# A choice of engine for each group in the token-wise half of a two-layer kernel

## The chip, the cores and the metric

One core of a Trainium2 chip runs the whole program. The metric is the device time of one launch in microseconds (us). Of the engines, PE is TensorE, DVE is VectorE, ACT is ScalarE, POOL is GpSimd and SP is SyncE, which only starts DMAs here.

## What is computed

Two transformer layers over 2048 tokens of 128 features, in float32. Between x and the output stand four residual blocks:

```python
x = x + attention(layernorm(x))        # 16 heads of 64, a dilated local mask
x = x + fp4_ffn(layernorm(x))          # gate, up and down, each with inputs and weights quantised
x = x + l1_attn(layernorm(x))          # see below
x = x + l1_ffn(layernorm(x))           # r, k, v with a mix of each token and the one before it

def fp4_quant_dequant(x):              # blocks of 16
    scale = max(max(abs(xb)) / 6, 1e-12)
    return GRID[searchsorted(MID, abs(xb / scale))] * sign(xb) * scale

# l1_attn: h1 = norm1_w * rms(x); q, k, v, a, g = in_proj(h1)
# q = rms over groups of 8; k = tanh(k); a = clip(sigmoid(a + 2), 0.6, 0.9995)
# states: a recurrence over the tokens with a and k * v, computed in chunks of 64
# y = sigmoid(g) * (q * states) + (1 - sigmoid(g)) * v; x = x + RES * out_proj(y)
# h2 = norm2_w * rms(x); x + RES * proj(silu(fc(h2)))
# l1_ffn: out = sigmoid(xr @ W_r) * (relu(xk @ W_k) ** 2 @ W_v)
```

## The kernel before

The program has two halves. The first is the attention block: 32 units (8 head pairs by 4 windows of 512 tokens) in a software pipeline over all engines. The second, the token-wise half, computes the other three blocks. It is cut into four groups g = 0 to 3 of 512 tokens (four tiles of 128), and every group runs the same chain of some 130 named steps, one or a few instructions each. A step is named in the code by a short name, and `h1(2)` is step h1 of group 2.

**Order.** There is no loop over the groups. Each engine has one list, written out by hand or by a planner, in which the steps of the four groups stand in the order in which the engine issues them, interleaved with the last attention units (28 to 31). An engine runs its list strictly in order: a step that waits holds up all behind it. The table `STEPS` names for each engine and group the steps in their order, so that `wait_for(e, name, g)` can turn a step's name into a semaphore's value. There is one semaphore for each engine and group.

**Steps, in the order of the data.** x1 adds attention's output; bn0 and ag0 take mean and variance; rs0 (POOL, four small instructions) makes the inverse deviation and, for ACT, its product with the negative mean; z0 (ACT, L1329) normalises four tiles of 128x128. Then comes the quantisation of x, qx0 to qx8 and xq, in which DVE, POOL and ACT take turns (maximum of a block, scale, reciprocal, product, exponent, rounding, scaling back). t2, xqt, gu0 to gu3, silu0 to silu3 and hm0 to hm3 are the gate and up products; qa and qb are the same quantisation of the two halves of their result; t3a, t3b, ht0 to ht2 and dn the down product; x2 the residual sum. bn1, ag1, rs1 and h1 (DVE, L1701, four instructions) normalise for l1_attn, rz1 and z2 (the same line) for the residual. pk, pv, pa, pg and pq are the five projections and th, v, ta, tg and q2 what ACT takes from them; a1 (DVE, L1613) clips a; aa and mk follow on ACT; p, f and s are the recurrence (two scans, L1618 and L1631); u, gv and w are products on POOL (L1794, L1799, L1803); rq, rx and trx make q's scale; e1, qn, m and y (L1657) build y. op, x3 and sq, rs3, h2 (DVE, L1720, four instructions) and t5, h2t lead to fc0 to fc3, mt0 to mt3 and pr; x23 (POOL, L1815) and x5 are residual sums; bn4, ag4, rs4, z3, t6, zt, xr, k, k1, k2, kv, r, sr, o0 and o (DVE, L1697) are l1_ffn; store writes 256 KB.

POOL's steps all work in SBUF; every step that reads or writes PSUM stands on DVE, ACT or PE.

Of the kernel before, what the change touches and what calls it, by code (L numbers as in the profile page):

```python
# [22 lines left out]
P = 128  # L23
# [80 lines left out]
def attention(nc, ctx, hidden, w_q, w_k, w_v, w_o, w_gate, w_up, w_down, plain_weights, columns, ident, constants,  # L104
# [146 lines left out]
    with nc.Block() as block:  # L251
# [106 lines left out]
        def _(pe):  # L358
# [171 lines left out]
            output(26); weigh(27, 0); weigh(27, 1); turn(28, 0); turn(27, 3); weigh(27, 2); scores(31, 0)  # L530
            weigh(27, 3); scores(31, 1); turn(28, 1); turn(28, 2); output(27); turn(28, 3); weigh(28, 0); weigh(28, 1)
            weigh(28, 2); weigh(28, 3); turn(29, 0); turn(29, 1); turn_weights(0); turn_weights(1); turn_weights(2)
            output(28); turn_weights(3); turn(29, 2); turn(29, 3); t1(0); turn_weights(4); turn_weights(5)
            turn(30, 0); turn_weights(6); weigh(29, 0); weigh(29, 1); weigh(29, 2); weigh(29, 3); turn(30, 2)
            turn_weights(7); output(29); turn(30, 1); turn(31, 0); weigh(30, 0); t1(1); turn(30, 3); weigh(30, 1)
            weigh(30, 2); weigh(30, 3); turn(31, 2); turn(31, 1); output(30); turn(31, 3); weigh(31, 0); weigh(31, 1)
            weigh(31, 2); t1(2); t2(0); weigh(31, 3); gu0(0); output(31); t1(3); gu1(0); t2(1); gu0(1); gu2(0); gu1(1)
            gu3(0); gu2(1); gu3(1); t2(2); gu0(2); t2(3); gu1(2); gu0(3); gu2(2); t3a(0); gu1(3); t3b(0); gu3(2)
            dn(0); gu2(3); t3a(1); t3b(1); dn(1); gu3(3); t4(0); pv(0); pk(0); pg(0); t3a(2); pa(0); t3b(2); pq(0)
            dn(2); t4(1); qq(0); pv(1); pk(1); t3a(3); pg(1); t3b(3); pa(1); pq(1); dn(3); t4(2); qq(1); pv(2); pk(2)  # L540
            trx(0); pg(2); pa(2); t4(3); pq(2); trx(1); pk(3); pv(3); op(0); pa(3); pg(3); qq(2); op(1); pq(3); t5(0)
            qq(3); trx(2); fc1(0); fc0(0); t5(1); fc3(0); fc2(0); fc1(1); fc0(1); trx(3); op(2); pr(0); fc3(1); fc2(1)
            op(3); t5(2); pr(1); fc0(2); fc1(2); t5(3); fc2(2); fc3(2); fc0(3); fc1(3); t6(0); pr(2); fc2(3); fc3(3)
            t6(1); k(0); pr(3); t6(2); k(1); k(2); r(1); kv(0); r(0); t6(3); r(2); kv(2); k(3); kv(1); r(3); kv(3)

        @block.scalar
        def _(act):
# [95 lines left out]
            for t in range(FIRST_STEP, DRAIN):  # L643
# [24 lines left out]
            th(2); tg(2); ta(2); h1t(3); q2(2); th(3); aa(2); v(3); mk(2); ta(3); sq(0); tg(3); rq0(2); q2(3); sq(1)
            h2t(0); aa(3); rq0(3); mt1(0); mt0(0); h2t(1); mk(3); mt3(0); mt2(0); mt0(1); sq(2); mt1(1); mt3(1)
            mt2(1); sq(3); h2t(2); mt0(2); mt1(2); h2t(3); mt3(2); mt2(2); mt0(3); zt_(0); xr0(0); mt1(3); mt2(3)  # L670
            mt3(3); zt_(1); xr0(1); zt_(2); xr0(2); k1(0); k2(0); k1(2); k2(2); k1(1); sr(1); sr(0); zt_(3); sr(2)
            xr0(3); k2(1); k1(3); k2(3); sr(3)
# [229 lines left out]
        def _(pool):  # L902
# [90 lines left out]
            qb1(2); qa1(3); qb3(2); qb4(2); qa3(3); rs1(0); rz1(0); qa4(3); hqa(2); hqb(2); qb1(3); qb3(3); qb4(3)  # L993
            rs1(1); rz1(1); hqa(3); hqb(3); u(0); rs1(2); rz1(2); gv(0); w(0); u(1); rx(0); rs1(3); gv(1); rx(1)
            rz1(3); w(1); u(2); gv(2); rs3(0); rx(2); rs3(1); w(2); u(3); gv(3); rx(3); w(3); rs3(2); x23(0); x23(1)
            rs3(3); rs4(0); rs4(1); x23(2); rs4(2); x23(3); rs4(3)

# [927 lines left out]
```

## Time and profile before

| | us |
|---|---|
| median of 3 runs | 507.01 (506.64 to 511.37) |
| time of the profiled execution | 503.8 |
| its span, first to last instruction | 501.9 |
| PE busy | 450.3 |
| DVE busy | 429.1 |
| ACT busy | 326.5 |
| POOL busy | 311.2 |

Busy times are sums over the whole span. The token-wise half fills the time from about 340 us on, and before that the attention half holds all engines. The last attention unit and the first steps of group 0 overlap from 334 to 357 us.

### The profile page before, as it was taken

The page shows a single profiled execution, that of the slowest core. Times are in us where ns is not written, and L with a number is a line of the kernel's source. Part 1 is how long each engine was busy: PE and PEld are TensorE (multiplying, and loading weights), DVE is VectorE, ACT ScalarE, POOL GpSimd, SP SyncE. Part 2 cuts the span into 40 slices and gives each one's busy share as a digit, 9 for nine tenths or more (in the row PEclk, how much of TensorE's full clock was granted, in tenths as well). Part 3 has the DMA queues.
Part 4 walks back from the last instruction along what each step waited for, and adds up shares of the span by engine and source line. Part 5 has one row for each costly group of instructions (what it writes and reads, how often), then busy time and mean ns, then how long its engine had stood idle before and what let it go on. Part 6 is the DMA issues. An engine that isn't in the chain of part 4 may idle for free.

```text
span 501.9 us, 17236 instructions
## 1 busy us (share of the span) xinstructions
PE 450.3 (90%) x6418; PEld 349.3 (70%) x6418; DVE 429.1 (86%) x1375; ACT 326.5 (65%) x953; POOL 311.2 (62%) x501
## 2 busy tenths in 40 slices
PE   0899799999999999999999999989859897878996
PEld 0677688878878778778878778867425655436765
DVE  4887478897899999999999878968898989899665
ACT  3477568778777677678678687755735467473544
POOL 4125348686577577577577675747678877765330
PEclk9999989999999999999999999999978999889999
DMA  6277862364352353443464455550000000000002
GB/s 209 105 226 204 205 220 49 69 127 96 71 121 60 74 110 64 88 99 84 91 135 104 85 127 100 110 101 2 1 0 0 2 0 1 1 1 2 1 0 84
DMA packets 136098, 40.52 MB, mean 81 GB/s; under 512 B 104976, under 2 KB 131024, under 8 KB 136016
## 3 DMA queue, kind: packets, MB, share of 16 engines
q1 hardware_dynamic: 135440, 38.38, 33.2%
q8 instruction: 51, 0.84, 0.7%
q10 hardware_dynamic: 576, 1.05, 0.6%
q14 instruction: 31, 0.25, 0.2%
HBM read 29.44 MB, written 9.96 MB: 79 GB/s over the span
## 4 chain that ended last, share of the span: by engine, by line
PE 52%; DVE 28%; issue 6%; POOL 5%; DMA 5%; ACT 3%; SPq 1%; DVEq 0%; ACTq 0%; POOLq 0%
PE psum L410 8%; PE psum L452 8%; PE psum L1159 5%; DVE pband L696 4%; PE psum L472 4%; PE psum L486 3%; PE psum L498 3%; PE psum L391 3%; PE psum L483 3%; DVE pt L757 2%; PE psum L393 2%; PE psum L392 2%; PE psum L376 2%; PE psum L1186 2%; DVE arena L769 1%
## 5 line engine op out<-in xcount | busy, mean ns | idle before, releaser
L928 POOL TENSOR_SCALAR pband<-pband,fac 128x192 f32<-128x192 f32 x256 | 104.0, 427 | 90.9 <-DVE fac L748 87.3
L555 ACT ACTIVATE pband<-pband,st 128x192 f32<-128x192 f32 x256 | 113.2, 448 | 0.3 <-DVE st L696 0.3
L696 DVE CUSTOM_DVE_ANT_0 pband<-psum,band_mask 128x192 f32<-128x192 f32 x256 | 76.1, 353 | 0.1
L410 PE MATMUL psum<-keys,q_class 64*64 64x192 f32 (+2 forms) x1536 | 66.4, 275 | 0.0
L452 PEld LDWEIGHTS psum<-ident,pband 128*128 128x128 f32 x384 | 46.1, 143 | 22.8 <-issue 13.4
L410 PEld LDWEIGHTS psum<-keys,q_class 64*64 64x64 f32 x1536 | 57.6, 133 | 2.5 <-issue 2.5
L452 PE MATMUL psum<-ident,pband 128*128 128x128 f32 x384 | 54.2, 278 | 3.5 <-ACT arena L626 2.8
L910 POOL COPY keys<-k_rows 128x512 f32<-128x512 f32 x32 | 36.5, 1140 | 25.6 <-issue 13.0
L555 ACT ACTIVATION_READ_ACCUMULATOR pband<-pband,st 128x1 f32 x256 | 49.4, 193 | 0.0
L757 DVE COPY pt<-psum 128x512 f32<-128x512 f32 x64 | 43.8, 684 | 2.3 <-PE psum L452 2.1
L571 ACT COPY pt<-psum 128x512 f32<-128x512 f32 x64 | 37.2, 581 | 7.2 <-PE psum L452 7.1
L918 POOL COPY q_class<-q_rows 128x512 f32<-128x512 f32 x32 | 36.1, 1127 | 7.7 <-ACT q_rows L595 7.7
L1154 PE MATMUL psum<-xt,arena 128*128 128x512 f32 x72 | 37.8, 649 | 1.1 <-ACT xt L1387 1.0
L937 POOL TENSOR_TENSOR pseg<-pseg,fac 128x512 f32<-128x512 f32 x32 | 34.1, 1066 | 2.9 <-DVE fac L748 2.8
L486 PE MATMUL psum<-pt,v_seg 64*64 64x64 f32 x1024 | 35.5, 218 | 0.0
L472 PE MATMUL psum<-pt,v_both 128*64 128x128 f32 x512 | 35.2, 279 | 0.0
L472 PEld LDWEIGHTS psum<-pt,v_both 128*64 128x64 f32 x512 | 27.3, 136 | 11.2 <-issue 11.2
L498 PE MATMUL psum<-o_sb,wo 128*128 128x512 f32 x64 | 32.9, 596 | 2.1 <-ACT o_sb L579 2.1
L391 PE MATMUL psum<-xn_hi,w_hi 128*128 128x512 f32 x64 | 31.0, 484 | 4.1 <-DVE arena L769 4.1
L410 PE MATMUL psum<-k_rows,q_rows 64*64 64x64 f32 x1024 | 32.7, 224 | 1.7 <-issue 1.7
L486 PEld LDWEIGHTS psum<-pt,v_seg 64*64 64x64 f32 x1024 | 32.6, 135 | 0.4 <-issue 0.2
L718 DVE TENSOR_REDUCE st<-pseg 128x8 f32<-128x512 f32 x32 | 21.9, 684 | 12.6 <-ACT pseg L563 12.4
(209 smaller groups left out, 1116.5 us busy)
## 6 DMA issues: line engine op xcount, KB each, us to landing
v_rows_dram<-arena SPq DMA_DIRECT2D x32, 256.0 KB, 2.9
v_both<-v_rows_dram SPq DMA_DIRECT2D x32, 256.0 KB, 3.8
v_seg<-v_rows_dram SPq DMA_DIRECT2D x64, 128.0 KB, 3.7
v_side<-v_rows_dram SPq DMA_DIRECT2D x96, 64.0 KB, 2.5
w_rows_dram<-st SPq DMA_DIRECT2D x64, 8.0 KB, 2.9
st<-w_rows_dram SPq DMA_DIRECT2D x64, 8.0 KB, 2.5
arena<-_attn_hidden_states_dram SPq DMA_DIRECT2D x4, 256.0 KB, 3.5
out_dram<-x SPq DMA_DIRECT2D x4, 256.0 KB, 2.3
```

Of the source, the lines that this page charges most:

```text
L391: pe.matmul(shared_bank[:, :], hi, xn_hi[:, cols], start=True, stop=False)
L410: return pe.matmul(bank[2 * r + head][rows, at:at + y.shape[1]], x, y, start=True, stop=True, skip_group_check=True)
L452: last = pe.transpose(turn_bank[odd][:, P * k:P * (k + 1)], src, ident[:, :])
L472: last = pe.matmul(by_class[dims, c, :], v_both[:, c, w, dims], turned[:, P * k:P * (k + 1)], start=(b == 0 and k < 2), stop=False, skip_g ...
L486: last = pe.matmul(out_bank[dims, cols], v_seg[dims, 2 * (TW * w + k) + half, :], turned[dims, cols], start=False, stop=(k == 3 and half = ...
L498: pe.matmul(shared_bank[:, :], wo[:, U // NW, :], o_sb[:, :], start=True, stop=True).then_inc(s_mix, 1)
L555: act.activation(x, x, ACT.Exp, bias=mine[:, head:head + 1], scale=-1.0, accum_out=mine[:, 2 + head:3 + head]).then_inc(s_exp, 1)
L571: act.copy(pt[:, PT_SLOTS + e % PT_SLOTS, :], turn_bank[1][:, :]).then_inc(s_pt[1], 1)
L696: dve.tensor_tensor_reduce(pband[:, G % P_SLOTS, c, head, :], bank[2 * r + head][:, at:at + BAND], band_mask[:, (0, 1, 1, 2)[w], SEG * (1 ...
L757: dve.tensor_copy(pt[:, e % PT_SLOTS, :], turn_bank[0][:, :]).then_inc(s_pt[0], 1)
L928: pool.tensor_scalar(x, x, fac[:, F % 2, 1, c, head:head + 1], 1.0, ALU.mult, ALU.mult).then_inc(s_scaled, 1)
L1154: end(pe.matmul(bk(g, to)[:, :], w, x, start=True, stop=True, skip_group_check=True), g, "tensor")
```

## The change

Before, a step stood on the same engine in all four groups. Now some steps have a version on a second engine, and each group picks one. Where the picks differ from before:

| step | before, all groups | after: group 0 | 1 | 2 | 3 |
|---|---|---|---|---|---|
| z0 | ACT | DVE | DVE | ACT | ACT |
| qx1, qx3 (128x32) | POOL | DVE | POOL | POOL | POOL |
| hqb | POOL | POOL | POOL | DVE | POOL |
| ht2 | ACT | ACT | ACT | DVE | ACT |
| h1 | DVE | ACT | ACT | ACT | ACT |
| z2 | DVE | ACT | DVE | ACT | ACT |
| gv | POOL | DVE | DVE | POOL | POOL |
| a1 | DVE | POOL | POOL | POOL | POOL |
| aa | ACT | ACT | ACT | DVE | ACT |
| w | POOL | POOL | POOL | DVE | POOL |
| y | DVE | POOL | DVE | POOL | POOL |
| x23 | POOL | POOL | DVE | POOL | DVE |
| h2 | DVE | DVE | DVE | ACT | DVE |
| h2t | ACT | DVE | ACT | ACT | ACT |
| zt | ACT | ACT | DVE | ACT | ACT |
| k1, k2 | ACT | DVE | ACT | ACT | ACT |
| o | DVE | POOL | POOL | DVE | DVE |

A norm that ACT makes needs two more small POOL instructions (the negative mean and its product), and one that DVE makes doesn't. So rs1 has four instead of two in all groups, rz1 in groups 0, 2 and 3, and rs0 two instead of four in groups 0 and 1. The step xr0 now waits for zt and not for t6. The lists of all four engines are written anew, the part around the last attention units too. What is computed stays the same. A cut of the diff:

```diff
 STEPS = {
...
     "vector": (
-        "x1 bn0 ag0 qx0 qx2 qx5 qx7 qx8 hm0 hm1 qa0 hm2 qa2 hm3 qb0 qb2 qa5 qb5 qa7 qb7 qb8 qa8 x2 bn1 ag1 "
-        "h1 a1 z2 p e1 f s rq qn m y x3 h2 x5 bn4 ag4 z3 xr o0 o",
...
+        "x1 bn0 ag0 z0 qx0 qx1 qx2 qx3 qx5 qx7 qx8 hm0 hm1 qa0 qa2 hm2 qa5 hm3 qb0 qb2 qa7 qb5 qa8 qb7 qb8 "
+        "x2 bn1 ag1 gv p e1 f s rq qn m x3 h2 h2t x5 bn4 ag4 z3 k1 k2 xr o0",
...
-SIGNALS = {"rs0": 4, "rs1": 2, "rz1": 2, "rs3": 2, "rs4": 2, "store": 16}
+SIGNALS = {"rs3": 2, "store": 16}
+
+AFFINE = {"rs0": "z0", "rs1": "h1", "rz1": "z2", "rs4": "z3"}
+
+def signals(g, name):
+    if name in AFFINE:
+        return 4 if AFFINE[name] in STEPS["scalar"][g].split() else 2
+    return SIGNALS.get(name, 1)
...
@@ in scalar(act)
+        def h1(g):
+            wait_for(act, "rs1", g)
+            token_norm(g, hb[g], x_rows[g], 0)
...
         def xr0(g):
-            wait_for(act, "t6", g)
+            wait_for(act, "zt", g)
...
@@ in vector(dve)
-        def h1(g):
-            wait_for(dve, "rs1", g)
-            token_norm(g, hb[g], x_rows[g], 0)
...
+        def gv(g):
+            wait_for(dve, "tg", g)
+            wait_for(dve, "v", g)
+            end(dve.tensor_tensor(slot(g, 8), slot(g, 3), slot(g, 1), ALU.mult), g, "vector")
...
@@ in gpsimd(pool)
+        def inverse_deviation(g, name, stats, which=0, factor=1.0, eps=LN_EPS):
+            wait_for(pool, stats, g)
+            full = signals(g, name) == 4
+            end(pool.tensor_scalar(rs[g][:, which, :], mv[g][:, :, 1], factor, eps, ALU.mult, ALU.add), g, "gpsimd")
+            if full:
+                end(pool.tensor_scalar(neg[g][:, which, :], mv[g][:, :, 0], -1.0, 1.0, ALU.mult, ALU.mult), g, "gpsimd")
+            wait_for(pool, name, g, 1)
+            end(pool.tensor_tensor(rs[g][:, which, :], rs[g][:, which, :], c["minus_half"][:, 0:GT], ALU.pow), g, "gpsimd")
+            if full:
+                wait_for(pool, name, g, 3)
+                end(pool.tensor_tensor(nm[g][:, which, :], neg[g][:, which, :], rs[g][:, which, :], ALU.mult), g, "gpsimd")
...
+        def a1(g):
+            wait_for(pool, "ta", g)
+            end(pool.tensor_scalar(slot(g, 2), slot(g, 2), 0.2, 0.999, ALU.max, ALU.min), g, "gpsimd")
...
@@ the list of DVE, a piece
-            qa7(2); qb5(2); qa8(2); h1(0); qb7(2); hm3(3); qb8(2); x2(1); qa5(3); qb0(3); bn1(1); qb2(3); qa7(3)
-            ag1(1); qa8(3); qb5(3); a1(0); h1(1); qb7(3); x2(2); qb8(3); z2(0); bn1(2); z2(1); ag1(2); p(0); e1(0)
-            f(0); h1(2); a1(1); s(0); rq(0); x2(3); bn1(3); e1(1); ag1(3); rq(1); p(1); qn(0); h1(3); m(0); f(1); y(0)
...
+            qb0(3); qb7(2); qb8(2); hqb(2); qb2(3); qa5(3); gv(0); qb5(3); qa7(3); ht2(2); qa8(3); qb7(3); qb8(3)
+            p(0); x2(2); bn1(2); ag1(2); e1(0); gv(1); f(0); e1(1); s(0); rq(0); x2(3); bn1(3); ag1(3); rq(1); qn(0)
+            m(0); p(1); f(1); s(1); x3_(0); qn(1); m(1); y(1); aa(2); z2(1); x3_(1); h2(0); p(2); h2t(0); h2(1); rq(2)
...
@@ the list of POOL, a piece
+            qb3(2); qa1(3); qb4(2); qa3(3); hqa(2); qa4(3); rs1(1); qb1(3); rz1(0); qb3(3); qb4(3); u(0); a1(0); w(0)
+            hqa(3); hqb(3); rz1(1); rs1(2); a1(1); rx(0); u(1); rs1(3); y(0); rx(1); w(1); a1(2); u(2); rs3(0); rz1(2)
```

## Rows read from the trace of the kernel before

**Rows 1.** The page: busy time, and busy tenths in 40 slices.

```profile
PE 450.3 (90%) x6418; PEld 349.3 (70%) x6418; DVE 429.1 (86%) x1375; ACT 326.5 (65%) x953; POOL 311.2 (62%) x501
PE   0899799999999999999999999989859897878996
DVE  4887478897899999999999878968898989899665
```

**Rows 2.** Windows, busy us of each engine, by stages of the token-wise half.

```profile
core 0: us, PE busy (x) PEld busy (x) DVE busy (x) ACT busy (x) POOL busy (x), PEclk, DMA share, GB/s
349.00:399.00 50.00, 39.57 (x220) 26.00 (x216) 44.80 (x94) 24.47 (x47) 37.39 (x53) 0.90 0.00 1
399.00:463.00 64.00, 53.10 (x262) 33.13 (x260) 60.32 (x112) 37.96 (x83) 47.05 (x44) 0.95 0.00 1
463.00:502.00 39.00, 34.45 (x216) 26.44 (x216) 24.32 (x74) 18.39 (x41) 9.30 (x12) 1.00 0.09 27
```

**Rows 3.** Chain that ended last, pieces (start, us), 399 to 498 us.

```profile
408.76 0.43 DVE hb L1701 x2
...
412.07 3.07 DVE z L1701 x4
...
429.76 1.15 DVE hb L1701 x3
...
433.71 1.49 DVE area L1613
...
453.87 1.92 DVE z L1701 x4
...
460.32 2.83 DVE hb L1720 x4
463.20 0.66 PE psum L1150 x4
...
497.69 0.70 DVE x L1692
```

**Rows 4.** DVE busy in line L1701 (h1, z2) by windows.

```profile
396.00:398.00 2.00, 1.11 (x4) 1.00 0.00 0
411.90:415.20 3.30, 3.15 (x4) 1.00 0.00 0
428.00:431.00 3.00, 2.31 (x4) 0.50 0.00 0
453.80:455.90 2.10, 1.99 (x4) 1.00 0.04 8
```

**Rows 5.** Single lines on DVE: duration in ns, min/median/max.

```profile
L1701 DVE TENSOR_SCALAR z<-arena,mv,rs x16: 326/335/1404, 412.0 to 463.8; 128x128 f32<-128x128 f32 x16
L1720 DVE TENSOR_SCALAR hb<-x,rs x16: 273/280/1299, 441.7 to 468.3; 128x128 f32<-128x128 f32 x16
L1613 DVE TENSOR_SCALAR area<-area x4: 401/417/1489, 408.2 to 440.4; 128x512 f32<-128x512 f32 x4
L1657 DVE TENSOR_TENSOR area<-area x4: 621/692/1756, 432.0 to 459.6; 128x512 f32<-128x512 f32 x4
```

**Rows 6.** Groups by form, 345 to 502 us, and one stretch of ACT's timeline.

```profile
L1533 DVE SCALAR_TENSOR_TENSOR area<-area 128x704 f32<-128x704 f32 x4 | 3.4, 856 | 0.0
L1692 DVE SCALAR_TENSOR_TENSOR x<-area,psum 128x512 f32<-128x512 f32 x4 | 2.7, 687 | 3.2 <-PE psum L1159 3.1
L1744 POOL TENSOR_TENSOR nm<-neg,rs 128x4 f32<-128x4 f32 x3 | 0.6, 203 | 0.2
338.85 1.65 ACT L1329 ACTIVATE z<-arena,nm,rs 128x128 f32<-128x128 f32 x4
```

**Rows 7.** POOL: single lines, and its busiest window.

```profile
L1815 POOL TENSOR_TENSOR arena<-arena,x x4: 1259/1266/1620, 459.8 to 480.4; 128x512 f32<-128x512 f32 x4
L928 POOL TENSOR_SCALAR pband<-pband,fac x256: 414/425/458, 46.3 to 342.0; 128x192 f32<-128x192 f32 x128
420.00:430.00 10.00, 6.73 (x28) 3.82 (x27) 8.72 (x21) 4.44 (x8) 9.75 (x9) 0.89 0.01 2
```

More of the change, by code:

```diff
@@ L895, in _ @@
[L895 to L899 removed]
+            (clear, x1, bn0, ag0, z0, qx0, qx1, qx2, qx3, qx5, qx7, qx8, hm0, hm1, hm2, hm3, qa0,
+             qa2, qa5, qa7, qa8, qb0, qb2, qb5, qb7, qb8, hqb, ht2, x2, bn1, ag1, z2, aa, p, f, s,
+             gv, w, rq, e1, qn, m, y, x3_, x23, h2, h2t, x5, bn4, ag4, z3, zt_, xr, k1, k2, o0, o) = tail_vector(dve)
@@ L991, in _ @@
-            qx4(2); qa3(0); qa4(0); qx1(3); qx3(3); qx4(3); qa1(1); qb1(0); xq(2); qa3(1); qb3(0); qb4(0); qb1(1)
-            xq(3); shift_weights(); qa4(1); qb3(1); qb4(1); hqb(0); hqa(0); qa1(2); qa3(2); hqa(1); qa4(2); hqb(1)
-            qb1(2); qa1(3); qb3(2); qb4(2); qa3(3); rs1(0); rz1(0); qa4(3); hqa(2); hqb(2); qb1(3); qb3(3); qb4(3)
-            rs1(1); rz1(1); hqa(3); hqb(3); u(0); rs1(2); rz1(2); gv(0); w(0); u(1); rx(0); rs1(3); gv(1); rx(1)
-            rz1(3); w(1); u(2); gv(2); rs3(0); rx(2); rs3(1); w(2); u(3); gv(3); rx(3); w(3); rs3(2); x23(0); x23(1)
@@ L1063, in wait_for @@
         engine, before = place[g][name]
-        e.wait_ge(done[engine, g], before + (signal or SIGNALS.get(name, 1)))
+        e.wait_ge(done[engine, g], before + (signal or signals(g, name)))
     def end(ins, g, engine):
@@ L1431, in sq, with h2 @@
             end(last, g, "scalar")
+        def h2(g):
+            wait_for(act, "rs3", g)
+            for a in range(GT):
+                last = act.activation(hb[g][:, a, :], x3[g][:, a, :], ACT.Copy, scale=rs[g][:, 0, a:a + 1])
+            end(last, g, "scalar")
         def h2t(g):
@@ L1537, in qx0, with qx1, qx3 @@
             largest(g, "x", "z0")
+        def qx1(g):
+            scaled(g, "x", "qx0")
         def qx2(g):
             inverted(g, "x", "qx1")
+        def qx3(g):
+            shortened(g, "x", "qx2")
         def qx5(g):
@@ L1855, in qb3, with o, y @@
             shortened(g, "b", "qb2")
-        return (shift_weights, rs0, qx1, qx3, qx4, xq, qa1, qa3, qa4, hqa, qb1, qb3, qb4, hqb, rs1, rz1, u, gv,
-                w, rx, x23, rs3, rs4)
+        def o(g):
+            wait_for(pool, "o0", g)
+            end(pool.tensor_tensor(flat(x3[g]), flat(x3[g]), flat(x_rows[g]), ALU.add), g, "gpsimd")
+        def y(g):
+            wait_for(pool, "m", g)
+            wait_for(pool, "w", g)
+            end(pool.tensor_tensor(slot(g, 4), slot(g, 4), slot(g, 8), ALU.add), g, "gpsimd")
+        def a1(g):
+            wait_for(pool, "ta", g)
+            end(pool.tensor_scalar(slot(g, 2), slot(g, 2), 0.2, 0.999, ALU.max, ALU.min), g, "gpsimd")
+        return (shift_weights, rs0, qx1, qx3, qx4, xq, qa1, qa3, qa4, hqa, qb1, qb3, qb4, hqb, rs1, rz1, u, a1,
+                gv, w, rx, y, x23, rs3, rs4, o)
     def sync(sp):
```

221 lines of the change are left out of this document (125 added, 96 removed), and 26 rows, old and new, of the table STEPS.

## The prediction

> **What bounds the kernel now.** I read the page first, then windows by stage, then the chain of waits, then single lines on DVE. On the page no engine is full: PE 90%, DVE 86%, ACT 65% and POOL 62% [rows 1]. The change leaves the body of the attention half alone, so only the time after 334 us counts, and there the windows show three stages [rows 2]. From 463 us on PE is the bound: the chain runs through PE without a gap from 463.20 to 497.69 us, then two DVE instructions and the last store [rows 3]. From 349 to 463 us it is DVE: 44.80 us busy in 50.00 and 60.32 in 64.00, so 8.9 us idle in 114. PE is idle for 10.4 + 10.9 = 21.3 us there, ACT for 51.6 and POOL for 29.6 [rows 2]. So up to 463 us PE waits for what DVE hands it, and each us by which DVE gets through its list earlier can start the last PE stretch a us earlier, up to 21 us. ACT has the most room.
>
> The reader should see a second thing in the rows: part of DVE's busy time is waiting. One z2 instruction takes 335 ns at the median and 1404 at most, one h2 280 and 1299, one a1 417 and 1489, one y 692 and 1756 [rows 5]. The four instructions of a norm overlap and take 1.11 us undisturbed, but 3.15, 2.31 and 1.99 us at three places [rows 4], and those places stand in the chain of waits: 3.07 us of z2(0) at 412, 1.15 of h1(3), 1.49 of a1(2), 1.92 of z2(2), 2.83 of h2(2) [rows 3]. These are instructions with SBUF operands only. One that reads PSUM is steady: four of them (L1692, o0) have a mean of 687 ns [rows 6]. The Trainium skill has a rule for that: "SBUF — State Buffer", section "Who interferes with whom", says that DVE and GpSimd take one pair of ports in turn, as a lock for a whole instruction, where DVE runs in a 2-port mode or has two inputs in SBUF. The maxima above agree, each about one POOL instruction longer than the median; what the rule would make of this change is the second rival.
>
> **What leaves DVE ahead of x5(0).** All of it lies in the stretch that DVE bounds.
> - h1 in four groups: 1.11 us in groups 0 to 2, as the first row of line L1701 shows for group 0, and 2.31 in group 3 [rows 4]: 5.6 us.
> - z2 in groups 0, 2 and 3: 3.15 + 1.99 + 1.1 = 6.2 us [rows 4].
> - a1 in four groups: 1.49 once and three times about 0.41, 2.7 us [rows 5].
> - y in groups 0, 2 and 3: 1.76 + 0.69 + 0.62 = 3.1 us [rows 5].
> - h2(2): 2.83 us in the chain, 2.9 with its overlap [rows 3].
>
> Sum 20.5 us. Undisturbed the same steps would be 4 x 1.11 + 3 x 1.1 + 4 x 0.40 + 3 x 0.62 + 4 x 0.28 = 12.3 us. So 8.2 us of the 20.5 are stretching, a factor of 1.67.
>
> **What comes to DVE.** None of these forms but z0 stands on DVE before, so I take the nearest rows: for gv(0), gv(1), w(2) and x23(1), two SBUF inputs of 128x512, y's median of 0.69 [rows 5], 2.8 us; for hqb(2), 128x704, 0.86 [rows 6]; for h2t(0) and ht2(2), which read PSUM, 0.69 each [rows 6], 1.4; for aa(2), an SBUF form like a1's, 0.42 [rows 5]; z0 twice as a norm of 1.11 [rows 4], 2.2; qx1(0) and qx3(0), 128x32 elements, at most 0.28, what 128x128 takes [rows 5], and I take 0.2 each, 0.4. Sum 8.1 us undisturbed. The SBUF forms, 6.3 of it without the small ones, can be stretched by the same 1.67, to 10.5; then it is 12.3 with the PSUM and small ones. DVE's balance ahead of x5(0) is 12.3 - 20.5 = -8.2 us. Bounds: no stretching of what comes gives 8.1 - 20.5 = -12.4; all stretching stays, only met by other instructions, gives 8.1 - 12.3 = -4.2. I take -8.2, the middle: POOL is no emptier than before (below), but fewer SBUF instructions of DVE are there to meet it.
>
> **What comes to ACT.** h1 four times, z2 three times, h2 once: 8 x 1.65 us as z0 takes on ACT [rows 6] is 13.2; z0 leaves twice, h2t, ht2 and aa once before 463 us, about 3.3 + 2 = 5.3. So +8 us against 51.6 idle: hidden as work. In the chain of one group it is not: h1 takes 1.65 instead of 1.11, and rs1 gets two small POOL instructions of 0.20 [rows 6], 0.5 together. That is +1.0 us from ag1 to h1 for each group. The cover would be gone if ACT stood in the chain for longer than it does now.
>
> **What comes to POOL.** a1 four times: at least 0.43, what 192 elements take, and at most the 1.26 of a product of 512 [rows 7]; I take 0.75, nearer the one-input row, 3.0 us. y three times 1.26, 3.8. Small instructions: seven norms get two (0.20 each, 0.5 for both with what lies between their starts, an estimate), two norms lose them, +2.5. Away go gv twice, w and x23(1), 4 x 1.26 = 5.0, hqb, 1.26 x 704 / 512 = 1.7, and the small qx1(0) and qx3(0), 0.4. Balance 9.3 - 7.1 = +2.2 us against 29.6 idle [rows 2], but between 420 and 430 us POOL is busy for 9.75 of 10 [rows 7]. In a group's chain y costs 1.26 instead of 0.69, and a1 0.75 instead of 0.42: +0.9. The Trainium skill speaks against these moves: "GPSIMD Engine Reference", section "Engine selection", has elementwise work on VectorE, since a two-input operation is about twice as slow on GpSimd. The rows agree with 1.26 against 0.69 (1.8 times) [rows 5, 7]; by the page's factor y would cost 1.38, 0.12 more, and the sum is the same.
>
> **Handing back.** One group's longer chain is +1.0 + 0.9 = 1.9 us. The groups are interleaved, so that is paid about once, where the last group feeds op. I add half of a POOL instruction (0.6) for a step held in a queue by what stands before it: 2.5 us.
>
> **After x5(0).** o(0), o(1) go to POOL, k1, k2 and zt(1) to DVE, x23(3) too. DVE has 14.7 of 39 us idle there and POOL 29.7 [rows 2], PE sets the pace and its matmuls are the same: 0. If the cover were gone, o on POOL would cost 0.57 more for one group, but group 3's, the last, stays on DVE. The new lists also start t2(0) and gu0(0) ahead of the last attention products, and put the last output of attention later. PE has 10.4 us idle between 349 and 399 to take that in [rows 2], and I price it at 0.
>
> **The sum.** -8.2 + 2.5 = -5.7 us against the profiled execution's 503.8 us (span 501.9): 498.1. The runs' median is 507.01, 3.2 above that execution, so I predict 507.0 - 5.7 = 501.3 us.
>
> **Rivals.**
> - *The work goes, the whole stretch with it.* DVE's balance is -12.4 and the longer chains are hidden by other groups: 507.0 - 12.4 = 494.6, at best. For it: PE's 21.3 us of idle time. Against: POOL goes on sharing with DVE.
> - *The stretching stays.* POOL's work grows by 2.2 us, and DVE still has z2(1), h2(0), h2(1), h2(3) and the new gv, w, hqb and x23 to meet it; the 8.2 us find other instructions. Then -4.2 + 2.5 = -1.7: 505.3 us, within 1%. It is what the lock rule of the Trainium skill's page named above would give, if each POOL instruction always finds one of DVE's. For it: one y, with two SBUF inputs as gv, w and x23 have, took 1.76 us [rows 5]. Against: 36 instructions of a form that meets POOL (norms, a1, h2) leave DVE and 9 come, beside five with two SBUF inputs.
> - *Slower: POOL's queue holds the recurrence.* a1 and y are now handed through POOL, whose list has w(0), which waits for DVE's gv(0), ahead of hqa(3), hqb(3), rs1(2) and a1(1). If each of the four a1 and three y waits for one POOL instruction at its longest (1.62 [rows 7]) and takes its own longer time (0.33 and 0.57), 11.3 + 1.3 + 1.7 = 14.3 us come back, with the norms' 1.0 and the -8.2 it is +7.1: 514.1 us. Three of the seven holds (4.9) eat the gain; the 1% is passed from six on. For it: 9.75 of 10 us busy [rows 7]. Against: POOL is idle for 29.6 us in the stretch [rows 2], and not every hand-over stands in the chain.
> - *The moves do nothing,* since PE's list or another group's chain bounds in their place: 507, within 1%.
>
> **Chances.** About 1% is what a measurement of this kernel can tell from no change (5.1 us: 501.9 and 512.1). The forecast, with its own range of 498 to 504.5, has 0.45, of which 0.3 lies below 501.9; the full relief has 0.15; the stretching that stays 0.13; nothing 0.12; POOL's queue 0.15, and it reaches 512.1 in nearly all of its cases. So faster by over 1% 0.3 + 0.15 and a little of the third case's scatter, 0.47; slower 0.15; within 1% 0.38. The range may leave out 2 in 10: half of POOL's queue above 511 and what is left of the best case below 495 (its 494.6 is a bound). So 495 to 511.
>
> **What would show it.** DVE's busy time between the first quantisation and x5(0) is lower by 4 to 12 us, line L1701's maxima on DVE are rarer, and PE's unbroken last stretch begins at 457 to 459 us and not at 463.2, and lasts 34 us as before. ACT's busy time between 349 us and that point rises by about 8 us and POOL's by 2. The prediction is wrong if PE's last stretch begins where it did although DVE is emptier: then what DVE waits for just before (a POOL y, an aa on ACT) names the rival. It is wrong too if the stretch is longer, or if DVE's idle time grows by what its work lost.

## The result

The changed kernel took 515.72 us (median of four runs, 513.32 to 515.98) against 507.24 us: a ratio of 1.0139 with a 95% interval of 1.0078 to 1.020. It is slower by about 1.4%, where 501.3 us and "faster" were forecast. Its profiled execution took 515.7 us, with a span of 514.0; that of the kernel before took 503.8 and 501.9. So the two executions compared below are 12.1 us apart in span and the medians 8.5: a few us of what the traces show is scatter.

The page of the changed kernel: busy times, busy tenths of PE and DVE in 40 slices, and the granted clock.

```profile
PE 457.6 (89%) x6418; PEld 355.7 (69%) x6418; DVE 420.9 (82%) x1357; ACT 331.4 (64%) x970; POOL 317.8 (62%) x512
PE   0899799999999999999999999778858998897996
DVE  4887478888899999999999788759887984987474
PEclk9999989999999999999999999989957996999999
```

Against [rows 1], DVE is busy for 8.2 us less, as the change meant it, ACT for 4.9 and POOL for 6.6 more. PE is busy for 7.3 us more with the same 6418 matmuls: it ran them at a lower granted clock (mean 0.964, before 0.980). From 321 to 360 us PE's tenths are 7, 7 and 8; the same three slices of the kernel before have 9, 8 and 9.

Windows of the changed kernel by the same stages, with the same columns as [rows 2].

```profile
349.00:399.00 50.00, 39.45 (x272) 25.26 (x271) 41.64 (x89) 23.13 (x43) 30.46 (x48) 0.83 0.00 1
399.00:463.00 64.00, 57.75 (x270) 38.75 (x268) 52.05 (x102) 43.30 (x93) 54.88 (x64) 0.92 0.00 1
463.00:502.00 39.00, 34.73 (x220) 26.48 (x219) 26.33 (x74) 20.59 (x55) 17.53 (x20) 1.00 0.00 1
```

From 399 to 463 us DVE has 52.05 us of work where it had 60.32, and it is idle for 12 us instead of 3.7. That was meant to bring PE's last stretch forward, and it didn't. POOL has 54.88 where it had 47.05. The granted clock is 0.83 from 349 to 399 us and 0.92 from 399 to 463, where it was 0.90 and 0.95.

Pieces of the chain that ended last in the changed kernel, 418 to 510 us (start, us).

```profile
418.75 2.45 POOL area L1946
...
422.56 3.64 POOL area L1829 x2
...
441.91 1.26 POOL area L1942
...
446.42 1.92 POOL area L1946
...
460.92 2.18 POOL area L1946
...
471.08 1.27 POOL area L1942
472.39 4.73 PE psum L1170 x40
...
477.60 0.70 ACT xt L1460
...
505.69 3.58 PE psum L1170 x32
509.30 0.70 DVE x L1728
```

L1946 is a1, now on POOL, and L1942 is y. The chain of before has DVE in nearly every piece shown [rows 3]. Summed over its pieces, the chain from 399 us to PE's last stretch has 35.0 us of DVE, 19.1 of POOL and none of PE before (64 us), and 5.1 of DVE, 37.1 of POOL and 16.2 of PE after (73 us). Three of the four a1 stand in it, with 6.55 us; three at DVE's median of 0.42 [rows 5] would be 1.3. PE's last stretch begins at 472.39 and not at 463.20, and ends at 509.27 and not at 497.69. It is 2.4 us longer too (36.9 against 34.5): it holds 224 matmuls where it held 216, and one wait of 0.7 us for ACT.

Single lines of the changed kernel: duration in ns, minimum/median/maximum, and who waited for a1.

```profile
L1737 DVE TENSOR_SCALAR z<-arena,mv,rs x12: 333/346/1295, 344.1 to 450.5; 128x128 f32<-128x128 f32 x12
L1761 DVE TENSOR_SCALAR hb<-x,rs x12: 274/278/515, 451.5 to 478.6; 128x128 f32<-128x128 f32 x12
L1340 ACT ACTIVATE hb<-arena,nm,rs x16: 479/482/494, 404.3 to 443.2; 128x128 f32<-128x128 f32 x16
L1942 POOL TENSOR_TENSOR area<-area x3: 1260/1264/1266, 441.9 to 471.1; 128x512 f32<-128x512 f32 x3
L1946 POOL TENSOR_SCALAR area<-area x4: 1919/2082/2450, 418.8 to 460.9; 128x512 f32<-128x512 f32 x4
  ACT area L1430: 3.1, 2
```

In these lines x12 or x4 is the number of instructions. y is as forecast. a1 isn't: 1.92 to 2.45 us on POOL, where the forecast had 0.75 with an upper bound of 1.26 [rows 7], and where DVE took 0.42 at the median [rows 5].

The seam, where the last attention unit and the first steps of group 0 overlap, also moved. From DVE's timeline in the changed kernel: the sums of unit 31 (L719), x1(0) (L1514), a copy and the first step of differences(31) (L728), with the idle time ahead of it in brackets.

```profile
333.87 0.67 DVE L719 TENSOR_REDUCE st<-pseg 128x8 f32<-128x512 f32 x1
...
335.06 0.68 DVE L1514 TENSOR_TENSOR arena<-arena,psum 128x512 f32<-128x512 f32 x1
...
336.97 0.66 DVE L758 COPY pt<-psum 128x512 f32<-128x512 f32 x1
342.56 0.19 DVE L728 TENSOR_REDUCE joint<-st 128x16 f32<-128x32 f32 x1 [4.93 <-DMA st<-w_rows_dram]
```

What SP's queue waited for in the changed kernel from 318 to 345 us (us in total, times, longest).

```profile
SPq L1053 <- DVE st L719: 2.6, 1, 2.6
```

The sums, x1(0) and the first step of differences(31) in the kernel before.

```profile
329.47 0.68 DVE L718 TENSOR_REDUCE st<-pseg 128x8 f32<-128x512 f32 x1
...
333.53 0.69 DVE L1489 TENSOR_TENSOR arena<-arena,psum 128x512 f32<-128x512 f32 x1 [0.18 <-PE psum L1150]
...
337.25 0.19 DVE L727 TENSOR_REDUCE joint<-st 128x16 f32<-128x32 f32 x1 [1.71 <-DMA st<-w_rows_dram]
```

The last attention unit sends its sums through DRAM and reads them back. In the changed lists the sums stand behind factors(30) and accumulate(28), so SP sends them later, and DVE sits idle for 4.93 us, not 1.71, with all of groups 1 to 3's first steps behind it. x1(0) ends 1.5 us later than before (335.74 against 334.22). x1(1) starts 6.4 later; in the new list it stands behind the wait and also behind z0(0), qx1(0), qx3(0) and qx5(0), which the old list didn't have there.

### The profile page after: what moved, and what is told of

Its sections match the earlier page's. It is cut to its first block, busy times and chain, and to the rows that moved or that the text cites. A ratio compares the mean times of both kernels' runs of the same rounds, so it can differ in the third digit from the quotient of the medians.

```text
span 514.0 us, 17246 instructions
## 1 busy us (share of the span) xinstructions
PE 457.6 (89%) x6418; PEld 355.7 (69%) x6418; DVE 420.9 (82%) x1357; ACT 331.4 (64%) x970; POOL 317.8 (62%) x512
## 4 chain that ended last, share of the span: by engine, by line
PE 47%; DVE 27%; POOL 8%; issue 7%; DMA 6%; ACT 3%; SPq 2%; DVEq 0%; ACTq 0%; POOLq 0%
PE psum L410 7%; PE psum L452 6%; DVE pband L697 5%; PE psum L1170 5%; DVE pt L758 3%; PE psum L472 3%; PE psum L391 3%; PE psum L483 2%; PE psum L486 2%; PE psum L498 2%; DMA w_rows_dram<-st 2%; PE psum L1165 2%; PE psum L1197 2%; PE psum L393 2%; PE psum L392 2%
## 5 line engine op out<-in xcount | busy, mean ns | idle before, releaser
L1165 PE MATMUL psum<-xt,arena 128*128 128x512 f32 x72 | 35.1, 610 | 3.0 <-ACT area L1422 1.0
L602 ACT ACTIVATE ediff<-diff 128x32 f32<-128x32 f32 x32 | 7.3, 228 | 43.9 <-DVE diff L732 43.9
L498 PE MATMUL psum<-o_sb,wo 128*128 128x512 f32 x64 | 34.0, 613 | 1.2 <-ACT o_sb L579 1.1
```

What stands on the lines that cost most here:

```text
L498: pe.matmul(shared_bank[:, :], wo[:, U // NW, :], o_sb[:, :], start=True, stop=True).then_inc(s_mix, 1)
L1165: end(pe.matmul(bk(g, to)[:, :], w, x, start=True, stop=True, skip_group_check=True), g, "tensor")
```

## The experiments

Each kernel's ratio is against the kernel before on the same chip, whose median is in the third column. The chips differ by up to 2.3 us in it, so across rows the ratios count and not the medians. The last column is worked out from the kernel's timeline: the time from the end of x1(0) to the end of the last kv product, which leaves out the attention half and its scatter (one execution each).

| kernel | median, us | before there, us | ratio (95%) | x1(0) to last kv, us |
|---|---|---|---|---|
| before | 507.2 to 509.5 |  | 1 | 163.4 |
| the change | 515.72 | 507.24 | 1.0139 (1.0078 to 1.020) | 173.5 |
| order_only | 523.45 | 508.16 | 1.0294 (1.0245 to 1.0342) | 180.7 |
| place_only | 513.83 | 508.16 | 1.0101 (1.0067 to 1.0135) | 171.0 |
| front_old | 513.53 | 508.40 | 1.0125 (1.0082 to 1.0169) | 168.9 |
| after_early | 513.70 | 508.16 | 1.0112 (1.0069 to 1.0156) | 170.1 |
| before_late | 511.27 | 508.16 | 1.0054 (1.0020 to 1.0087) | 165.6 |
| z2_act | 507.48 | 508.40 | 0.9985 (0.9950 to 1.0019) | 163.3 |
| h1_act | 509.72 | 508.40 | 1.0020 (0.9983 to 1.0056) | 166.3 |
| a1_y_pool | 514.39 | 508.40 | 1.0157 (1.0097 to 1.0216) | 171.8 |
| a1_pool | 514.01 | 507.64 | 1.0110 (1.0062 to 1.0158) | 168.6 |
| y_pool | 508.31 | 507.64 | 0.9999 (0.9962 to 1.0036) | 164.0 |
| a1_pool_mult | 507.33 | 507.64 | 1.0004 (0.9966 to 1.0042) | 164.2 |
| a1_pool_max | 515.99, one run | 507.18 |  | 172.1 |
| after_a1_dve | 510.15 | 507.64 | 1.0046 (1.0018 to 1.0073) | 167.8 |
| early_a1_dve | 508.62 | 507.18 | 1.0009 (0.9977 to 1.0042) | 167.9 |
| picks_no_a1 | 515.17 | 507.18 | 1.0127 (1.0087 to 1.0167) | 169.7 |
| picks_no_front | 509.05 | 509.50 | 1.0006 (0.9968 to 1.0045) | 163.4 |
| relief_mix | 507.66 | 507.18 | 0.9985 (0.9953 to 1.0018) | 166.9 |
| relief_h1 | 510.26 | 509.50 | 1.0025 (0.9988 to 1.0062) | 166.1 |

### Order and picks apart

```diff
  # place_only: each engine's list as before, moved steps put in by their time
  #   DVE: ... factors(31); z0(0); ...        POOL: ... rs1(1); a1(0); rz1(1); ...
  # order_only: the change's lists, every step on its engine of before
```

place_only:

> The engines of the change with the order of the kernel before: every moved step stands in its new engine's list where the trace of before has its start; z0(0) stands right behind factors(31). My forecast's sum (DVE relieved by 8.2 us, 2.5 handed back) gives 507 - 5.7 = 501. Theory B (POOL's queue holds a1 and y): 511 to 514. Theories A and C (the seam or the order cost the time, the picks themselves don't): 501 to 507.

order_only:

> The order of the change with the engines of the kernel before: every moved step stands back on its old engine, where the trace of after has its start; h1 and a1 on DVE again. Theory C (the order costs): 514 to 520, as the change or worse, since DVE has its old work again. Theory A (only the seam's three steps): about 512. Theory B (the engines cost): about 507.

In the old order the picks cost about 5.7 us (513.83 against 508.16); in the new order they gain 7.7 (523.45 to 515.72; by the ratios 1.0294 to 1.0139). Neither part is good alone. The new order was written for the new picks, and without them it is the worst kernel of all; the picks lose in either case against the kernel before.

front_old has the change's picks with the old order up to dn, and the new one behind it:

```diff
-            bn1(1); ag1(1); qb0(3); ...     # the change's order only from x2 on
+            (all lists before x2 as in the kernel before, z0(0) behind factors(31))
```

> The engines of the change; up to the down product (x1 to dn) and around attention's last units the order of the kernel before, from x2 on the order of the change. If the new order of the first part (group 3's quantisation and gate-up behind the other groups', gu0(3) ends at 397.4 us and before at 381.5) is what costs: 505 to 508. If the order or the picks of the second part cost: 512 to 515.

It took 513.53 us, place_only 513.83 and after_early 513.70. So with all picks, a1 on POOL among them, three orders come out alike. That doesn't show that the order is indifferent. With a1 back on DVE the same picks have a ratio of 1.0127 in the old order and 1.0009 in the new one (picks_no_a1 and early_a1_dve, below).

### The exchange of unit 31

```diff
 # after_early (before_late is the reverse edit of the kernel before)
-            accumulate(27); differences(30); even_turned(29, 0); factors(30)
-            accumulate(28); seg_sums(31); even_turned(29, 2); x1(0)
+            accumulate(27); differences(30); seg_sums(31); even_turned(29, 0); factors(30)
+            accumulate(28); even_turned(29, 2); x1(0)
-            band_exps(31, 0); take_out(28); seg_exps(31); exp_difference(30); take_weights(0); band_exps(31, 1)
+            band_exps(31, 0); band_exps(31, 1); seg_exps(31); take_out(28); exp_difference(30); take_weights(0)
```

after_early:

> The kernel after the change with three steps of attention's last unit moved to where the kernel before has them: on DVE seg_sums(31) right behind differences(30), on ACT band_exps(31,1) and seg_exps(31) ahead of take_out(28) and the first take_weights. Theory A (the late exchange of unit 31's statistics delays everything, differences(31) starts at 342.56 us after the change and at 337.25 before): differences(31) returns to about 337 to 338 us and the time falls by some 5 us, to about 510.5. Theory B (POOL's queue holds a1 and y): no change beyond 1 us, about 515, since the seam's delay is taken up by waits later. Theory C (the new order of the groups, group 3 above all, is what costs): falls by 0 to 2 us.

before_late:

> The mirror of it: the kernel before with seg_sums(31) on DVE put behind accumulate(28) and band_exps(31,1) on ACT behind seg_exps(31), take_out(28) and take_weights(0), as after the change; nothing else. Theory A: differences(31) starts about 5 us later, near 342, and the time rises from 507 to about 511 or 512. Theories B and C: within 1 to 2 us of 507.

The early exchange takes 2.0 us off the changed kernel by the medians and 1.4 by the ratios (1.0139 to 1.0112), which the intervals don't tell apart. The late one costs the kernel before 0.54%, 2.7 us, with an interval that doesn't hold 1. In the traces differences(31) starts at 338.26 and not 342.56 in after_early, and at 340.55 and not 337.25 in before_late. So a late exchange costs in the old order, and in the new one I put it at 1 to 3 us, an estimate; the prediction had priced it at 0.

### What takes work from DVE

```diff
 # z2_act: z2(0), z2(2), z2(3), h2(2) to ACT.  h1_act: h1(0) to h1(3) to ACT.
 # relief_mix: z2_act's, y(0), y(2), y(3), o(0), o(1) to POOL.  relief_h1: relief_mix's and h1_act's.
+        def h1(g):
+            wait_for(act, "rs1", g)
+            token_norm(g, hb[g], x_rows[g], 0)
```

z2_act:

> The kernel before with four picks of the change alone: z2(0), z2(2), z2(3) and h2(2) on ACT, each where its start was in the order of before (and rz1's two more small POOL instructions for those groups). These norms took 3.15, 1.99, 1.1 and 2.9 us on DVE, 9.1 us, and z2 is wanted only by x3. If DVE's relief is worth what I forecast: 3 to 6 us off, 502 to 505. If relieving DVE is worth nothing in a fixed order, since what stands next waits for PE or POOL: 507 to 509. If each pick costs through waits in ACT's queue: over 510.

h1_act:

> The kernel before with h1 of all four groups on ACT, each where its start was, and rs1 with its two more POOL instructions. If the chain ag1, rs1, h1 is what the picks lengthen (0.5 us on POOL, 0.5 on ACT, and steps of ACT held behind a waiting h1): 509 to 512, and most of the +5.7 us of the run with all picks in the old order. If DVE's relief of 5.6 us counts: 503 to 506.

relief_mix:

> The kernel before with only those picks that take work from DVE and were free alone: z2(0), z2(2), z2(3) and h2(2) on ACT, y(0), y(2), y(3), o(0) and o(1) on POOL. Alone, the z2 and h2 picks gave 507.48 and the y picks 508.31 against 508.2 (no difference that the runs resolve). DVE loses some 9 us of busy time by it and takes on nothing. If DVE's list sets the pace between 349 and 463 us, as the prediction had it, most of that comes off: 500 to 503 us. If the chain of each group passes through DVE, ACT and POOL in turn and DVE's work counts only where it stands in that chain, 506 to 509, no difference.

relief_h1:

> The kernel with what leaves DVE and was free in sum (z2, h2, y, o: 507.66 us against 507.18) and h1 of all groups on ACT besides: all of the change that relieves DVE, except a1, in the order of the kernel before, with nothing coming to DVE. h1 alone gave 1.002. If the picks that leave DVE stay free together, 507 to 509. If h1 on ACT is in the way of the other norms there (its list is longer then by 13 us), 511 or more, and the cost of the picks without a1 (+8.0) is found here.

None of the four differs from the kernel before by an amount that the runs resolve. In relief_h1 most leaves DVE and nothing comes to it, and its window shows a relief greater than the one forecast.

```profile
399.00:463.00 64.00, 51.99 (x255) 32.82 (x255) 48.83 (x85) 44.37 (x101) 50.28 (x54) 0.95 0.00 1
```

DVE is busy for 48.83 us where it was for 60.32 [rows 2], 11.5 us less, and the time doesn't move (1.0025). PE's last stretch begins at 466.00 in it, 2.8 us later than before and not earlier. What stands in the chain of relief_h1 instead, pieces from 399 to 466 us:

```profile
411.22 0.66 PE psum L1152 x4
411.87 0.99 PE psum L1252 x8
412.87 1.83 PE psum L1156 x4
...
415.31 1.53 ACT z L1331 x4
...
434.46 2.18 POOL area L1941
...
452.15 5.13 PE psum L1156 x8
...
457.72 4.47 PE psum L1161 x40
...
464.68 1.28 ACT hb L1446 x4
466.00 0.66 PE psum L1152 x4
```

Summed over all its pieces from 399 to 463 us, this chain has 9.1 us of DVE, 7.2 of ACT, 21.3 of POOL and 18.8 of PE; that of before has 35.0, 1.8, 19.1 and none of PE. DVE has left the chain, and other work has filled it. Part of that are products on PE, the same as before. Part are the moved steps themselves: the 1.53 us of ACT are z2(0), and the 2.18 of POOL are y(0). So relief_h1 shows that relief and longer steps come to nothing in sum, and not what each is worth alone. z2_act is cleaner, since z2 is wanted only by x3 and h2(2) is the one other step that it moves: DVE's busy time falls by 6.7 us over the span (422.4 against 429.1), and the ratio is 0.9985.

Where some of z2_act's relief went can be seen in PE's timeline. Two pieces of the kernel before, then the same two of z2_act: the first waits for h2(1) on DVE.

```profile
450.18 0.66 PE L1150 MATMUL psum<-ident,hb 128*128 128x128 f32 x4 [2.20 <-DVE hb L1720]
450.67 3.60 PE L1154 MATMUL psum<-xt,arena 128*128 128x512 f32 x8
```

```profile
448.79 0.70 PE L1152 MATMUL psum<-ident,hb 128*128 128x128 f32 x4 [3.73 <-DVE hb L1760]
449.29 5.29 PE L1156 MATMUL psum<-xt,arena 128*128 128x512 f32 x8
```

h2(1) is ready 1.4 us earlier. But PE has waited 1.5 us longer for it, and takes 5.29 us for the eight products behind it where it took 3.60. Its granted clock is 0.70 from 448.79 to 454.57 us, and in the kernel before it was 1.00 from 450.18 to 454.27. The 40 products that come next on PE start at 454.85 us where they started at 454.55: at this place the clock has taken back what DVE gave. In relief_h1 the eight products take the same 5.29 us, at 0.71. These are single executions.

The kernel before had a sign of this from 349 to 399 us. Pieces of its chain there:

```profile
373.93 1.54 PE psum L1186 x2
...
387.52 2.92 PE psum L1159 x24
...
394.58 2.92 PE psum L1159 x24
```

Summed over all pieces of that stretch, the chain has 26.0 us of PE and 14.2 of DVE, although DVE was busy for 44.80 of 50 [rows 2].

A rule of the Trainium skill fits what the prediction did: "Perfetto Trace Analysis", section "Identifying the Most-Contended Engine", takes a VectorE's occupancy as a fair measure of its limit, and would optimise the engine with the highest occupancy first. Between 349 and 463 us that was DVE (105.1 of 114 us). The runs don't bear the rule out here: 11.5 us less of it, with the longer steps that this brought, were worth nothing.

### What goes to POOL

```diff
 # a1_y_pool: a1 of all groups and y(0), y(2), y(3).  a1_pool, y_pool: one of the two.
+        def a1(g):                                   # on POOL
+            wait_for(pool, "ta", g)
+            end(pool.tensor_scalar(slot(g, 2), slot(g, 2), 0.2, 0.999, ALU.max, ALU.min), g, "gpsimd")
 # a1_pool_mult: 1.0, 1.0, ALU.mult, ALU.mult        a1_pool_max: 0.2, 1.0, ALU.max, ALU.mult
```

a1_y_pool:

> The kernel before with a1 of all groups and y of groups 0, 2 and 3 on POOL, each where its start was. If POOL's queue holds the recurrence (the rival of the prediction): 510 to 514. If not: 505 to 508, DVE's 5.8 us of relief against 0.9 us of longer steps for each group.

a1_pool:

> The kernel before with a1 alone on POOL, in all groups, each where its start was. In the run with a1 and y on POOL a1 took 1.92 to 2.55 us there and not the 0.75 I took, against 0.42 on DVE. If a1's own length in the recurrence's chain is the cost: most of the +6 us of that run, 511 to 514. If y or the two together fill POOL's queue: 508 to 510.

y_pool:

> The kernel before with y(0), y(2), y(3) alone on POOL. If a1 is the cost: 507.5 to 509.5, three times 0.57 us longer with about one of them in the chain. If handing through POOL's queue is the cost whatever the step: 511 to 513.

a1_pool_mult:

> As the run with a1 alone on POOL, but the instruction multiplies twice by 1.0 instead of max with 0.2 and min with 0.999, so a isn't clipped; same size, same place, same waits. If POOL's max and min are what is slow: the instruction takes 0.6 to 1.1 us and the time falls to 507 to 509.5. If a one-input instruction of 512 elements takes 1.9 us on POOL whatever the operation: no change against the run with a1 alone on POOL.

a1_pool_max:

> The kernel before with a1 on POOL as one comparison and one product (the larger of a and 0.2, times 1.0), so a isn't clipped at 0.999. The form with two comparisons took 1.92 to 2.71 us for an instruction of 128x512, the form with two products 0.62 at the least. If each comparison adds the same, the least is 1.27 us. If the first or the pair is what is slow, it is 0.6 or 1.9.

y alone costs nothing that can be measured, 508.31 us. a1 alone costs 6.4 us, 514.01 against 507.64 (5.6 by the ratio 1.0110). Both together cost 6.0 (8.0 by the ratio), with intervals that overlap. And the same four hand-overs with two products in place of the two comparisons cost nothing, 507.33. That kernel leaves out the clip, so it computes something else and serves for the timing only. The lines of a1 on POOL in a1_pool, a1_pool_mult and a1_pool_max, in this order:

```profile
L1945 POOL TENSOR_SCALAR area<-area x4: 1918/2122/2710, 412.1 to 448.5; 128x512 f32<-128x512 f32 x4
```

```profile
L1945 POOL TENSOR_SCALAR area<-area x4: 617/985/1526, 408.5 to 441.5; 128x512 f32<-128x512 f32 x4
```

```profile
L1945 POOL TENSOR_SCALAR area<-area x4: 1923/2302/2827, 412.7 to 448.9; 128x512 f32<-128x512 f32 x4
```

Two products take 0.62 us at the least, a maximum and a product 1.92, a maximum and a minimum 1.92. So the instruction is slow with the maximum in it, and the minimum besides adds nothing; that each adds the same was one of the expectations and is wrong. A minimum alone was not tried. Shape, place in the queue, semaphores and what the instruction reads are the same in all three, so the cost of a1_pool is the instruction's own length and not the hand-over. a1_pool_max ran once (515.99 us), in line with a1_pool.

"GPSIMD Engine Reference" of the Trainium skill, section "Engine selection", has an operation with one input at roughly line rate on GpSimd. With two products the trace comes nearer to that (0.62 us, against 0.40 that DVE takes at the least for max and min [rows 5]). With max and min on both engines it differs: GpSimd takes 4.8 times as long as DVE, and there the measurement decides.

### a1 and the exchange, undone in the change

```diff
 # after_a1_dve: the change with a1 back on DVE.  early_a1_dve: after_early's edit besides.
-            ... qa5(3); gv(0); qb5(3); qa7(3); ht2(2)
+            ... qa5(3); gv(0); a1(0); qb5(3); qa7(3); ht2(2)
```

after_a1_dve:

> The kernel after the change with a1 of all groups back on DVE, each behind the time at which ta of its group ended; all other picks and the order stay. If a1 on POOL costs in the change what it costs in the old order: 515.7 falls by 4 to 6 us, to 510 to 512. If the change's own order hides a1: 514 to 516.

early_a1_dve:

> The changed kernel with both suspected costs undone: a1 of all four groups back on DVE, and unit 31's exchange as early as in the kernel before (its sums right behind differences(30) on DVE, its two exponentials ahead of take_out(28) and the weights on ACT). The changed kernel with only a1 returned took 510.15 us, with only the early exchange 513.7, as it stands 515.7. If the two costs add and are all there is (5.6 and 2.0), 508.1 us, within 0.3% of the kernel before. If the seam's cost was hidden or paid for by a1's, 510 as without it. If, with both gone, DVE's lower busy time between 349 and 463 us turns into time, as the prediction had it, 502 or less.

With a1 on DVE the changed kernel takes 510.15 us, 5.6 less (4.7 by the ratios, 1.0139 to 1.0046). With the exchange early too it takes 508.62, 1.5 less again, and its ratio of 1.0009 can't be told from 1; the second step lies within the intervals. So these two edits give the whole loss of 1.4% (7.1 us) back, a1 most of it. They don't make the kernel faster than the one before. All the rest of the change, its relief of DVE included, is worth nothing in sum. How much of that is relief and how much costs, in this order, no run says.

### What comes to DVE in front

If a1 were the whole cost of the picks in the old order too, taking it out there should give about 508.

```diff
 # picks_no_a1: place_only with a1 on DVE.  picks_no_front: also z0(0), z0(1) on ACT, qx1(0), qx3(0) on POOL
-            accumulate(30); z0(1); qx0(1); qx2(1); x1(2)       # DVE
+            accumulate(30); qx0(1); qx2(1); x1(2)
```

picks_no_a1:

> All picks of the change except a1, which stays on DVE in all groups, in the order of the kernel before. With a1 among them, the same picks in the same order took 513.83 us against 508.16 (+5.7). If a1 on POOL is the whole of that, 508 us, within 0.5% of before. If the other picks cost something of their own (ACT's longer norms, z0 and gv on DVE), 510 or more. If they relieve DVE and that counts once a1 is out of the way, 505 or less.

picks_no_front:

> The picks of the change without a1 and without the four steps at the front (z0(0), z0(1), qx1(0), qx3(0) stay on ACT and POOL), in the order of the kernel before. With those four it took 515.17 us against 507.18 (+8.0). Against the other kernel of this call it adds what comes to DVE later: hqb(2), ht2(2), aa(2), gv(0), gv(1), w(2), x23(1), x23(3), h2t(0), zt(1), k1(0), k2(0). If the front steps in DVE's list are the cost (x1 and z0(1) late), 509 or less; if the steps that come later are, 513 or more here and 508 in the other; if each is a part, between.

picks_no_a1 took 515.17 us, +8.0 by the medians and +6.4 by the ratio of 1.0127, where about 508 was possible, so in the old order a1 is not the only cost. Leaving the four front steps where they were gives all of it back (509.05, ratio 1.0006): they cost 1.2%, about 6 us. In picks_no_front, z0(1) on ACT and the pieces of the chain that hold gu0(1), then the copy xqt(1):

```profile
351.82 1.66 ACT L1332 ACTIVATE z<-arena,nm,rs 128x128 f32<-128x128 f32 x4
...
360.50 0.86 PE psum L1189 x2
361.36 0.61 PE psum L1190 x2
...
362.45 0.57 ACT xt L1356
```

The chain of picks_no_a1 at the same steps:

```profile
353.46 1.40 DVE z L1729 x4
...
361.65 1.23 PE psum L1189 x2
362.88 1.17 PE psum L1190 x2
...
364.95 0.59 ACT xt L1356
```

On ACT the norm ended at 353.48, just as DVE finished accumulate(30), and DVE took qx0(1) at once: the norm was hidden. On DVE it stands behind accumulate(30) and is in the chain for its 1.40 us. PE then comes to the same four products 1.15 us later and needs 2.40 us for them and not 1.47. Its granted clock is 0.58 over these products (361.6 to 364.1 us) and 1.00 in picks_no_front (360.4 to 362.0). Ahead of them PE was busy for 1.32 of 3.60 us (from 358.0) here, and for 1.34 of 2.40 there. So 1.4 us has become 2.5 by xqt(1) (2.0 counted from the end of x1(0), which is 0.5 later in this execution), and by the end 6.3 (169.7 against 163.4). The two costs don't add in the old order: place_only, with a1 on POOL and the front steps on DVE, took no more (513.83) than either alone. In the new order early_a1_dve has the front steps on DVE, and its sum is 1.0009. So they either cost nothing there or something else pays for them; neither was tried.

## Why the prediction was wrong

- **DVE's list.** In sum this was sized well. The prediction had -8.2 us ahead of x5(0), and with what comes and leaves behind it (k1, k2, zt(1) and x23(3) come, about 2.8; two o leave, 1.4) -6.8 in all; the page shows -8.2. The stretching went too: the maximum of an h2 instruction is 0.52 us (1.30 before), and only one z2 or z0 is long (1.30; before, the longest was 1.40) [rows 5]. In its parts the sum was not right, so some of the agreement is luck. For what leaves DVE in relief_h1 (h1, z2, h2, y and two o) the prediction's terms give 19.2 us (20.5 without a1, with 1.4 for o), and its page shows 15.0 (414.1 against 429.1). What comes was put at 12.3, and 2.8 behind x5(0), 15.1 in all; it comes to 7.8 (421.9 in picks_no_a1 against the same 414.1). These are single executions.
- **ACT.** One norm took 4 x 0.48 us, overlapped 1.65, as in [rows 6]. Over the whole span it is +4.9 us; +8 was forecast up to x5(0), less about 2 for k1, k2 and zt behind it.
- **POOL: the term that was mis-sized.** a1 was put at 0.75 us, "at least 0.43 ... and at most the 1.26 of a product of 512". The four took 1.92 to 2.45 us, 5.5 us more in sum than the 3.0 forecast. The upper bound came from a row of another operation, a product with two inputs; the lower one from a row with two products. Neither row had a comparison in it. a1 stands in each group's chain between ta and aa, and three of the four stand in the chain that ended last, so it costs 5 to 6 us in the change and alone. y at 1.26 was right, and moving it alone cost nothing.
- **"Each us by which DVE gets through its list earlier can start the last PE stretch a us earlier."** This step failed, and it carried the -8.2. relief_h1 took 11.5 us from DVE and its last PE stretch began 2.8 us later; z2_act took 6.7 from DVE over the span and changed nothing. The windows had shown PE idle for 21.3 us and DVE full, and the chain with DVE in it; neither says how far behind the next chain is. By the lower ends of the intervals of z2_act and relief_mix (-0.5%) the gain, less what the moved steps cost in their new places, is at most some 2.5 us. Two things stood against the step in the traces. The trace of before already showed the chain from 349 to 399 us with 26.0 us of PE and only 14.2 of DVE, so DVE's full list wasn't what held most of that part. And in z2_act the 1.4 us won at h2(1) were lost again to the granted clock.
- **The seam priced at 0.** "PE has 10.4 us idle between 349 and 399 to take that in" looked at PE, but what the new lists moved was the sums of unit 31 on DVE, with an exchange through DRAM behind them. It costs 2.7 us in the kernel before, and in the change 1.4 to 2.0, which the intervals don't resolve.
- **z0 on DVE counted in a balance.** 2.2 us of z0 and 0.4 of qx1(0) and qx3(0) at the front were set against relief 60 us later. In the old order these four steps cost about 6 us.
- **Handing back 2.5 us.** No run isolates it. relief_h1's +0.25% (interval -0.1 to +0.6%) bounds the sum of relief and longer chains, not each; so whether the forecast relief came and was handed back whole, or never came, stays open there.

Of the rivals, "slower: POOL's queue holds the recurrence" came nearest in number (514.1) and in place: the chain does pass through POOL's a1 and y, and ACT waited for a1. Its mechanism was not the one: it had the waits in POOL's queue as 11.3 of the 14.3 us that come back, and the four hand-overs of a1_pool_mult and the three of y_pool cost nothing. "The moves do nothing, since ... another group's chain bounds in their place" was right in sum for everything but a1 and the exchange. Both together are the result: a relief that brought nothing net, and about 7 us of cost.

No kernel here beats the one before. relief_mix and z2_act have the lowest ratios, 0.9985, with intervals that hold 1.

What stays open: whether the front steps are free in the new order or paid for by something else, what order and picks do to each other otherwise (the new lists with the old picks are at 1.0294, and no run takes that apart), why the costs of a1 and of the front don't add in the old one, and how large the scatter of a single span is in the last column of the table (relief_mix shows 3.5 us there that its twelve runs don't).

## What to carry to other kernels

An engine that is busy for 94% of a stretch and stands in the chain of waits is not yet worth relieving: ask what the chain would be without it, and test that first with one run that only takes work away. Bound the price of a moved instruction by a row with the same operation, not merely the same shape, and if there is none measure it alone: four instructions that took 1.7 us more each than on DVE cost 5 to 6 us. When lists are written anew, look first at the step that starts an exchange through DRAM, and at each step that leaves an engine where it was hidden.

## What the runs showed of the hardware

- On POOL a one-input instruction of 128x512 float32 took 0.62 us at the least with two products (a1_pool_mult) and 1.92 with max and a product (a1_pool_max) or max and min (a1_pool). DVE took 0.40 at the least for max and min [rows 5].
- The same matmuls took longer where the granted clock was lower. Four products took 1.47 us at 1.00 (picks_no_front) and 2.40 at 0.58 (picks_no_a1), behind a longer idle time of PE. Eight took 3.60 us at 1.00 (before) and 5.29 in z2_act, where the clock was 0.70 over them and the transposes beside them.
- PE's busy time over the whole span is no measure of the loss. It is 7.3 us higher in the change with the same matmuls, for a span 12.1 longer, but y_pool has 450.7 us in a span of 509.8 and the kernel before 450.3 in 501.9.
